# A decoder layer's cross-attention: ranks copied out of PSUM early, and ScalarE takes the transposed normed rows out of PSUM with scale and shift

## The reference

```
x = _layernorm(x + attn(x))                       # x1, then x1n
xn = layer_norm(ctx, gx, bx);  ln = layer_norm(x, gl, bl)
q = ln @ Wq * SCALE; k = xn @ Wk; v = xn @ Wv     # 8 heads of 64
out = softmax(q k^T) v @ Wo + bo
x = _layernorm(x + out)                           # x2
logits = x @ router_w.T                           # 8 experts
chosen_e = argmax(softmax(logits)); pos = rank of the token among those of its expert
kept = pos < C
```

## Time and profile before

| | us |
|---|---|
| runs timed (3): lowest, median, highest | 3839.96, 3845.3, 3853.6 |
| profiled execution: its own time | 3851.77 |
| its span, first to last instruction | 3849.8 |
| cross-attention, from the first projection's start to the last rank product's | 2229.75 to 2818.76 |
| chunks 1 to 7, together | 444.2 |
| share of the span with TensorE busy | 91% |
| mean granted TensorE clock | 0.948 of full |

### The profile page before, as it was taken

The page is one execution under the profiler, slowest core; times in us unless marked ns, Lnnn a source line. Parts: engine busy times, 40 slices in busy tenths (PEclk is TensorE's granted clock), DMA queues, the critical chain, the costliest instruction groups (busy, mean ns, idle before and its releaser), DMA issues. The chain is left out here.

```text
span 3849.8 us, 51828 instructions
## 1 busy us (share of the span) xinstructions
PE 3497.5 (91%) x18133; PEld 2299.5 (60%) x18134; DVE 2541.3 (66%) x4546; ACT 1735.2 (45%) x3066; POOL 2048.3 (53%) x1031
## 2 busy tenths in 40 slices
PE   7999999999999999999999768878759889899885
PEld 5455455454554554554544257767659778888875
DVE  5777777777777777777777157767534655565666
ACT  2555555555555555555555433322223433343342
POOL 1789898889888888888889700110110101100112
PEclk9999999999999999999999779989769899999998
DMA  6321312213222223131200031121132333223332
GB/s 213 99 60 51 101 51 83 78 52 96 60 72 88 64 65 97 47 100 56 69 12 15 28 110 57 68 90 55 44 118 72 104 110 108 98 88 111 116 116 97
DMA packets 190735, 309.76 MB, mean 80 GB/s; under 512 B 25609, under 2 KB 72329, under 8 KB 190490
## 3 DMA queue, kind: packets, MB, share of 16 engines
q1 hardware_dynamic: 164330, 238.58, 19.8%
q0 software_dynamic: 15072, 45.89, 3.4%
q10 hardware_dynamic: 11088, 22.02, 1.7%
HBM read 197.23 MB, written 61.33 MB: 67 GB/s over the span
## 5 line engine op out<-in xcount | busy, mean ns | idle before, releaser
L463 DVE TENSOR_REDUCE sa_part_max<-sa_mx 128x1 f32<-128x512 f32 x2048 | 1282.6, 680 | 545.5 <-PE sa_mx L574 541.5
L426 ACT ACTIVATE sa_prob<-sa_sc 128x512 f32<-128x512 f32 x2048 | 1122.2, 595 | 824.9 <-PE sa_sc L620 779.5
L247 POOL TENSOR_TENSOR sa_quad_sum<-sa_quad_sum,sa_prob 128x1024 f32<-128x1024 f32 x512 | 1209.5, 2401 | 7.1 <-ACT sa_prob L426 7.1
L574 PE MATMUL sa_mx<-sa_k_stack,sa_q_stack 96*128 96x512 f32 x2048 | 967.5, 474 | 28.8 <-DVE sa_part_max L463 15.9
L620 PE MATMUL sa_sc<-sa_q_stack,sa_k_stack 98*128 98x512 f32 x2048 | 865.8, 424 | 7.8 <-ACT sa_prob L426 7.7
L247 POOL TENSOR_TENSOR sa_quad_sum<-sa_prob 128x1024 f32<-128x1024 f32 x256 | 616.7, 2430 | 254.6 <-ACT sa_prob L426 254.6
L574 PEld LDWEIGHTS sa_mx<-sa_k_stack,sa_q_stack 96*128 96x128 f32 x2048 | 390.7, 191 | 378.7 <-issue 205.6
L620 PEld LDWEIGHTS sa_sc<-sa_q_stack,sa_k_stack 98*128 98x128 f32 x2048 | 389.1, 190 | 317.5 <-ACT sa_prob L426 273.3
L1838 PE MATMUL ex_h<-ex_xT,ex_w 128*128 128x384 f32 (+2 forms) x2688 | 468.8, 331 | 81.0 <-DVE ex_xT L1740 28.7
L1838 PEld LDWEIGHTS ex_h<-ex_xT,ex_w 128*128 128x128 f32 x2688 | 451.4, 196 | 106.1 <-issue 70.7
L589 PE MATMUL sa_pv<-sa_prob,sa_v 128*32 128x512 f32 x4096 | 504.2, 611 | 0.7 <-ACT sa_prob L426 0.7
(11 more groups left out here) (199 smaller groups left out, 3311.8 us busy)
## 6 DMA issues: line engine op xcount, KB each, us to landing
ex_w_in<-in_L_ffn_w_dram SPq DMA_DIRECT2D x130, 512.0 KB, 4.2
sa_xT<-xT SPq DMA_DIRECT2D x57, 1024.0 KB, 5.1
sa_q_stack<-sa_hilo SPq DMA_DIRECT2D x372, 64.0 KB, 2.0
sa_k_stack<-sa_hilo SPq DMA_DIRECT2D x360, 64.0 KB, 2.0
ex_xg<-rows POOLq DMA_DIRECT2D x54, 256.0 KB, 3.3
rows<-sa_empty SPq DMA_DIRECT2D x48, 257.0 KB, 3.7
ex_rows<-rows POOLq DMA_DIRECT2D x8, 1542.0 KB, 7.6
sa_prob<-in_x_dram ACTq DMA_DIRECT2D x8, 1024.0 KB, 7.3
```

What stands on the lines that cost most here:

```text
L247: pool.tensor_tensor(quad_sum[:, i % 2, heads, :], so_far, prob[:, k, heads, :], ALU.add).then_inc(quad_ready, 1)
L426: act.activation(prob[:, kt % 4, j, :], sc[n % 2][:, :], ACT.Exp, scale=SCALE).then_inc(prob_ready, 1)
L463: dve.reduce_max(part_max[:, q, j, k:k + 1], mx[n % 3][:, :], AX_X).then_inc(max_read, 1)
L574: pe.matmul(mx[n % 3][:, :], q_stack[0:QK, j, at:at + P], k_stack[0:QK, g // NQ % 2, j, k * BANK:(k + 1) * BANK], start=True, stop=True).t ...
```

## The change

1. A new tile `ranked`, and `read_ranks(n)`: one VectorE copy of ranks and counts out of bank 7, at the head of chunk n + 2 (before `highest`). `place_tokens` then reads `ranked`. `ROUTE_STEPS` goes from 21 to 22 and `RANKS_READ` from 13 to 7, the step of that copy.
2. The scale and shift of x1nT (PSUM to `whole`) goes from VectorE to ScalarE, as an Identity activation, interleaved with the high copies; and `high_x1nT(n + 1)` stands ahead of `norm1(n + 1)`.
3. In VectorE's list `add_bias(n + 2)` moves ahead of `low_p(n, 2)`, and `residual2` of tiles 0 and 1 moves ahead of `low_p` of tiles 2 and 3: residual 0, low 2, residual 1, low 3.
4. TensorE starts `project`, `scores` and `outputs` when the high parts are there, and waits for the low part of the moving side only ahead of the third product.

```
-        ROUTE_STEPS, LX_KNOWN, HOT_KNOWN, RANKS_READ = 21, 2, 6, 13
+        ROUTE_STEPS, LX_KNOWN, HOT_KNOWN, RANKS_READ = 22, 2, 6, 7
             def leave_x1nT(n):
-                for k in range(KC):
-                    dve.wait_ge(x1n_mm, n * KC + k + 1)
-                    dve.tensor_scalar(whole[:, k, :], bank[X1N_BANK[k]][:, :], gl[:, k:k + 1], bl[:, k:k + 1], ALU.mult, ALU.add).then_inc(xt_ready, 1)
                 for k in range(KC):
                     low(xt_hi, n * KC + k + 1, x1nT[:, 1, k, :], whole[:, k, :], x1nT[:, 0, k, :], x1nT_ready)
+            def read_ranks(n):
+                dve.wait_ge(rank_mm, n + 1)
+                then(dve.tensor_copy(ranked[:, :, :, :], bank[7][:, P:P + 2 * TQ * E].rearrange("p (i t e) -> p i t e", i=2, e=E)))
             def place_tokens(n):
-                dve.wait_ge(rank_mm, n + 1)
-                counts = bank[7][:, P + TQ * E:P + 2 * TQ * E].rearrange("p (t e) -> p t e", e=E)
-                ranks = bank[7][:, P:P + TQ * E].rearrange("p (t e) -> p t e", e=E)
                 for t in range(TQ):
-                    then(dve.tensor_tensor(placed[:, t + 1, :], placed[:, t, :], counts[:, t, :], ALU.add))
-                then(dve.tensor_tensor(at_tile[:, :, :], placed[:, 0:TQ, :], ranks, ALU.add))
+                    then(dve.tensor_tensor(placed[:, t + 1, :], placed[:, t, :], ranked[:, 1, t, :], ALU.add))
+                then(dve.tensor_tensor(at_tile[:, :, :], placed[:, 0:TQ, :], ranked[:, 0, :, :], ALU.add))
...
             for n in range(NCH):
                 more = n + 1 < NCH
+                if n >= 2:
+                    read_ranks(n - 2)
                 highest(n, 0)
...
-                low_p(n, 2)
                 if n + 2 < NCH:
                     add_bias(n + 2)
+                residual2(n, (0,))
+                low_p(n, 2)
+                residual2(n, (1,))
                 low_p(n, 3)
                 if n > 0:
                     choose(n - 1)
-                residual2(n, (0, 1))
...
             def high_x1nT(n):
                 act.wait_ge(s_mm, n * TQ)
                 for k in range(KC):
-                    act.wait_ge(xt_ready, n * KC + k + 1)
-                    act.activation(x1nT[:, 0, k, :], whole[:, k, :], ACT.Copy).then_inc(xt_hi, 1)
+                    act.wait_ge(x1n_mm, n * KC + k + 1)
+                    act.activation(whole[:, k, :], bank[X1N_BANK[k]][:, :], ACT.Identity, bias=bl[:, k:k + 1], scale=gl[:, k:k + 1]).then_inc(xt_ready, 1)
+                    if k > 0:
+                        act.wait_ge(xt_ready, n * KC + k)
+                        act.activation(x1nT[:, 0, k - 1, :], whole[:, k - 1, :], ACT.Copy).then_inc(xt_hi, 1)
+                act.wait_ge(xt_ready, (n + 1) * KC)
+                act.activation(x1nT[:, 0, KC - 1, :], whole[:, KC - 1, :], ACT.Copy).then_inc(xt_hi, 1)
...
                 if more:
+                    high_x1nT(n + 1)
                     norm1(n + 1)
-                    high_x1nT(n + 1)
...
             def scores(n):
-                pe.wait_ge(x1nT_ready, (n + 1) * KC)
+                pe.wait_ge(xt_hi, (n + 1) * KC)
...
             def outputs(n, t):
-                pe.wait_ge(pT_ready, n * TQ + t + 1)
+                pe.wait_ge(p_hi, n * TQ + t + 1)
...
                 for i, (pp, pw) in enumerate(PARTS):
+                    if pp == 1:
+                        pe.wait_ge(pT_ready, n * TQ + t + 1)
```

More of the change, by code:

```diff
@@ L735, in cross_attention @@
         lx, ex, hot, cand, at_tile = (s.sb(i, [P, TQ, E]) for i in ("lx", "ex", "hot", "cand", "at_tile"))
+        ranked = s.sb("ranked", [P, 2, TQ, E])
         placed = s.sb("placed", [P, TQ + 1, E])
@@ L1119, in choose @@
                 assert done[0] == n * ROUTE_STEPS + HOT_KNOWN
+            def read_ranks(n):
+                dve.wait_ge(rank_mm, n + 1)
+                then(dve.tensor_copy(ranked[:, :, :, :], bank[7][:, P:P + 2 * TQ * E].rearrange("p (i t e) -> p i t e", i=2, e=E)))
+                assert done[0] == n * ROUTE_STEPS + RANKS_READ
             def place_tokens(n):
@@ L1223, in _ @@
             norm2(NCH - 1)
+            read_ranks(NCH - 2)
             place_tokens(NCH - 2)
             choose(NCH - 1)
+            read_ranks(NCH - 1)
             place_tokens(NCH - 1)
@@ L1374, in project @@
                 if t == 0:
-                    pe.wait_ge(a_ready, (n + 2) * KC)
+                    pe.wait_ge(a_ready, KC)
+                    pe.wait_ge(a_hi, (n + 2) * KC)
                 if n <= 1 and t < 2:
@@ L1386, in project @@
                 for i, (pa, pw) in enumerate(PARTS):
+                    if t == 0 and pa == 1:
+                        pe.wait_ge(a_ready, (n + 2) * KC)
                     for k in range(KC):
@@ L1417, in scores @@
                         for i, (px, pw) in enumerate(PARTS):
+                            if t == 0 and half == 0 and px == 1:
+                                pe.wait_ge(x1nT_ready, (n + 1) * KC)
                             for k in range(KC):
```

## The result

The changed kernel takes 3780.01 us in the median of four runs (3777.68 to 3781.98), the kernel before in the same session 3847.49 (3839.96 to 3853.6): ratio 0.9825, interval 0.9806 to 0.9845, so 67.5 us less. Predicted were 3782 us, that is 63.2 less than the 3845.3 known then.

A forecast was written before the change was run, and what follows sets the result against it. TensorE's waits for `at_tile` ahead of the logits, and the lower clock behind them, bound the kernel. Chunks 1 to 7 -62.8, chunk 0 +2.0, start -2.4: -63.2 us, from 3845.3 to 3782, range 3763 to 3810.

The forecast's parts named there:

- The mechanism: TensorE waits for `at_tile` ahead of the logits, 45.9 us in six waits; with ranks copied early, logits run at once.
- the walk: The prediction's step-by-step times for chunk 3, then the other chunks against the trace of before; sum -63.2 us.
- 3 to 4 us a chunk: New waits of TensorE's x1nT transposes for `ca_pT`, 3 to 4 us a chunk, where 0.5 was.
- The load: Load of `xb` ahead of `add_bias`: lands 8.0 us after issue, 7.4 to 10.0; VectorE waits 1.2 in chunk 3.
- Above 10.0 nothing was seen: Said against a slower outcome (chance 0.015): the load of `xb` takes 8 to 10 us, never more in the trace.
- The clock, one fall of two: Low clock at both outputs: tile 0's take 5.3 us, not 3.71; the last two 8.7, not 7.19.
- three terms given for chunk 7: 5.1 idle ahead of the logits and 4.0 ahead of the last outputs go, 8.70 becomes 7.2: -10.4 us.
- Rival B: High clock kept through both halves, 1.6 us more in six chunks twice, -19: 3763; chance 0.10.
- Rival C: Clock falls early between outputs of tiles 1 and 2, last outputs 14.4 instead of 8.7, +34: 3816; chance 0.09.
- chunk 0: +2.0 us by VectorE's new order: a wait for `low_p(0, 2)` and a clock fall.
- Just in time: In chunk 3, low parts (`low_qk`) there at 2527 for scores(4) at 2527.6, held back 3.27 us before.
- Worth nothing by themselves: x1nT's scale and shift on ScalarE, covered by outputs of tiles 2 and 3; no gain except at `low_qk`, 3.27 us.

## Why the prediction was right

- **The mechanism held.** The wait for `at_tile` was the whole of TensorE's stop ahead of the logits: the copy alone removed it, everything else alone left it at 45.9 us. The copy takes 0.22 us (0.2 assumed).
- **The number is closer than the walk.** The walk was done on profiled executions, and these differ by 72.6 us where it gave 63.2, 9.4 more; 2.1 of that is self-attention's. That the medians, 3782 and 3780.0, come out within 2 us is in part luck: between medians the change is worth 67.5, and the median of before came out 2.2 us above the 3845.3 that the forecast started from.
- **The gain was given back where the walk put it.** The prediction said that TensorE would wait for `low_p(n, 2)`, behind the load of `xb` and its additions, and then for `low_p(n, 3)`. It does, for 15.4 and 5.7 us, 3.5 a chunk in chunks 1 to 6 ("3 to 4 us a chunk"), and moving `add_bias` away freed 27 us. The order alone was neutral, which the walk, that costed all parts of a chunk in one sum, had not said.
- **The load.** 1.2 us of waiting was forecast in a common chunk; in chunks 1 to 5 VectorE waited 4.35, 5.97, 1.54, 0.29 and 2.60. In chunk 2 the load was taken at 10.0 us and landed after 12.1: chunk 2 is 1.4 us longer than predicted. A store and a load of `wqk` were issued within a microsecond ahead of it in both kernels, so why it took 2.1 us longer is open. "Above 10.0 nothing was seen" held for the five loads of the earlier trace rows only: in the same trace the stage's first load of `xb` landed after 12.2. Issued ahead of the store, the five land in 5.1 to 6.3.
- **The clock, one fall of two.** The first outputs met the low clock in chunks 2 to 7 (5.29 to 6.45 us, 5.3 predicted; in chunk 7 it was low in the logits already, which took 6.83), but not in chunk 1 (3.73), the very place whose row in the trace of before the forecast leaned on. The second, 8.70 at the last outputs, was taken for each of chunks 1 to 5 and came whole in 1 and 5 (8.53, 8.54) and hardly in 2 (7.57), not in 3 and 4. That is most of why chunk 4 is 2.6 us under the forecast. Longer first outputs and shorter last ones nearly cancel, so the sum came out better than its terms; that is luck too. (The three terms given for chunk 7 add up to 10.6, not 10.4.)
- **Rival B, that the clock holds**, fell: in chunk 3 the record shows no idle time between the probabilities' transposes and the first outputs, and those ran at 0.54 all the same. By the Trainium skill (TensorE: Matmul & The Clock Gate, Part 1) the clock follows how busy TensorE has been lately; read as the prediction read it, with transposes and logits in one unbroken row counted as busy, the trace does not agree. Rival C, that the second half stretches to the low clock, was not seen in any chunk: the longest pair took 8.54 of the 14.4.
- **Mis-sized: chunk 0**, +2.0 predicted and -2.9 measured, the largest error of the sum. The step assumed a wait for `low_p(0, 2)` and a clock fall, on the pattern of later chunks. The waits came (0.94 and 1.33), but the last outputs stayed at full clock (7.20). And the first outputs start 58.8 us after scores(0) instead of 62.6, which the walk had not looked at: their own wait is 0.31 us instead of 1.81, two waits ahead are 0.5 shorter each (3.15 and 2.75 instead of 3.63 and 3.24), and half of the scores ran 1.2 faster (8.35 instead of 9.57), which no edit touches.
- **"Just in time" was not quite:** scores(4) waited 1.08 us for `low_qk` where none was predicted; it was 3.27 before. **"Worth nothing by themselves"**, of x1nT on ScalarE, looks too strict: undoing it cost 5 to 8 us, at the edge of what was resolved, with longer waits for `low_p`. That they are longer because the 2.9 us on VectorE push the next chunk's `low_p` back is argued, not shown.

Open: what makes the clock fall at the outputs of some chunks and not of others, with like rows ahead of them. So every sum here is uncertain by 1.5 to 2.7 us for each place where it can fall (8.70 against 7.19, 6.45 against 3.71).

## What to carry to other kernels

When a stall is taken away, walk the waiting engine's in-order list from that point and look for a DMA wait in it: `add_bias` started 11.5 us behind its load's landing before (2521.72 against 2502.20 + 8.0) and now arrives ahead of it, and whatever the critical engine needs that is queued behind it is late. Work without a near consumer, as `add_bias` here, goes behind that, or its load goes ahead of stores in the issuing queue. Both are ordering only; here the first was worth 27 us of 3780 and the second 14, and they were not tried together. Price an operation in the second half of a change against the schedule that the first half creates.

## What the runs showed of the hardware that was not expected

- TensorE's granted clock fell without idle time ahead of the fall. In chunk 3 of the changed kernel it did transposes (128x128) and logits (128x8) back to back, and then the first outputs ran at 0.54, mostly at the lower of the two levels (1.2 against 2.4 GHz): 6.45 us where 3.71 is the time at full clock. With the logits whole and ahead of them, the first outputs kept full clock in one of chunks 1 to 6 in the changed kernel, in one with `add_bias` late, and in two with the probabilities first. With the logits moved away or cut in pieces they kept it in six of six. So work of this kind ahead of wide products makes a fall likely, not certain. What the DMA engines did at the time does not sort the cases: in chunk 1 of the changed kernel the first outputs ran at 1.00 with a DMA share of 0.97, in chunk 6 at 0.68 with 0.52.
- ScalarE's Identity with a scale and a shift per partition, 128x512 out of PSUM, took 0.78 us; the copy of the same shape between SBUF tiles 0.62. In a row they overlap: the copy starts 0.68 us after the Identity (2505.46 and 2506.14). The 0.73 of the prediction was such a distance from start to start, so it was rather too high than too low.
